# Second layer's state-input projection in four column tiles, its three-way split on 128 columns, the parts spread by small DMAs, a two-input multiply by D, and new instruction orders

## The reference, cut to what matters

```python
xn = _layernorm(x);  x = x + attention(xn) + mixture_of_experts(xn)      # first layer
xn = _layernorm(x);  x = x + state_space(xn) + gated_mlp(xn)             # second layer

def state_space(x, W_in, conv_w, conv_b, A_log, D, W_x, W_dt, b_dt, W_out):
    xs, z = split(x @ W_in)                      # 256 channels each
    xs = silu(causal_conv(xs, conv_w) + conv_b)
    dt = softplus(xs @ W_dt + b_dt)
    Bs = xs @ W_x                                # 16 states per token
    def step(h, inp):                            # h: 256 channels x 16 states
        dt_t, Bs_t, x_t = inp
        h = h * exp(-exp(A_log) * dt_t[..., None]) + Bs_t[:, None, :]
        return (h, sum(h, axis=-1) + D * x_t)
    y = scan(step) * silu(z)
    return y @ W_out
```

## Time and profile before

| what | value |
|---|---|
| device time, median of 3 runs | 382.94 us |
| span of the profiled execution (first to last instruction) | 381.6 us |
| instructions | 5772 |
| TensorE busy | 368.0 us (96%) |
| ScalarE busy | 317.8 us (83%) |
| VectorE busy | 303.0 us (79%) |
| GpSimd busy | 252.4 us (66%) |
| granted TensorE clock | 1.000 of full speed |

### The profile page before, as it was taken

The page is one execution under the profiler, slowest core; times in us unless marked ns, Lnnn a source line. Parts: engine busy times, 40 slices in busy tenths (PEclk is TensorE's granted clock), DMA queues, the critical chain, the costliest instruction groups (busy, mean ns, idle before and its releaser), DMA issues.

```text
span 381.6 us, 5772 instructions
## 1 busy us (share of the span) xinstructions
PE 368.0 (96%) x1762; PEld 184.9 (48%) x1762; DVE 303.0 (79%) x508; ACT 317.8 (83%) x541; POOL 252.4 (66%) x293
## 2 busy tenths in 40 slices
PE   7999999999999999999998899999999999899996
PEld 5667535455545453333344334654445544374545
DVE  4877878878788879469999589989999879686850
ACT  4924879787879887899999799999999999999450
POOL 2245814614515111636899983999999999999880
PEclk9999999999999999999999999999999999999999
DMA  5273875734555310000000000000000000000000
GB/s 208 74 163 117 164 188 157 130 58 103 154 114 120 73 24 3 2 0 1 0 0 3 1 0 0 2 27 1 1 2 0 0 28 3 0 0 1 29 0 27
DMA packets 27726, 18.84 MB, mean 49 GB/s; under 512 B 2832, under 2 KB 26672, under 8 KB 27440
## 3 DMA queue, kind: packets, MB, share of 16 engines
q1 hardware_dynamic: 27696, 18.48, 20.0%
HBM read 13.29 MB, written 4.98 MB: 48 GB/s over the span
## 4 chain that ended last, share of the span: by engine, by line
PE 40%; issue 33%; POOL 13%; ACT 9%; DVE 4%; DMA 1%; POOLq 1%; ACTq 0%; DVEq 0%
POOL acc L1212 9%; PE bank L361 7%; PE bank L346 5%; PE bank L332 5%; PE bank L392 4%; PE bank L400 4%; DVE hb L1157 3%; ACT da L1082 3%; ACT pt L552 3%; PE bank L455 2%; PE bank L321 2%; PE bank L461 1%; PE bank L928 1%; POOL y L1220 1%; PE bank L418 1%
## 5 line engine op out<-in xcount | busy, mean ns | idle before, releaser
L1212 POOL TENSOR_TENSOR acc<-acc,hb 128x512 f32<-128x512 f32 x128 | 158.3, 1268 | 22.1 <-DVE hb L1157 17.5
L1157 DVE TENSOR_TENSOR_SCAN hb<-da,bank 128x512 f32<-128x512 f32 x128 | 146.3, 1201 | 22.6 <-PE bank L864 17.8
L593 DVE TENSOR_REDUCE mx<-bank 128x2 f32<-128x512 f32 x128 | 83.6, 685 | 22.4 <-PE bank L332 18.5
L552 ACT ACTIVATE pt<-bank 128x512 f32<-128x512 f32 x128 | 71.4, 596 | 16.2 <-PE bank L346 13.8
L1082 ACT ACTIVATE da<-dt,nega 128x510 f32<-128x510 f32 x128 | 82.5, 714 | 0.2
L903 PE MATMUL bank<-gelu,ld 128*128 128x512 f32 x128 | 58.3, 593 | 1.1 <-ACT gelu L1063 1.1
L891 PE MATMUL bank<-sil,ld 128*128 128x512 f32 x128 | 58.7, 594 | 0.0
L346 PE MATMUL bank<-q_st,k_st 51*128 51x512 bf16 x128 | 42.4, 383 | 1.5 <-ACT pt L552 1.3
L332 PE MATMUL bank<-k_st,q_st 48*128 48x256 bf16 x240 | 39.3, 273 | 0.0
L903 PEld LDWEIGHTS bank<-gelu,ld 128*128 128x128 f32 x128 | 24.0, 190 | 27.8 <-issue 26.0
L891 PEld LDWEIGHTS bank<-sil,ld 128*128 128x128 f32 x128 | 23.9, 190 | 25.4 <-issue 24.0
(11 more groups left out here) (149 smaller groups left out, 565.2 us busy)
## 6 DMA issues: line engine op xcount, KB each, us to landing
q_st<-q_scr SPq DMA_DIRECT2D x8, 384.0 KB, 4.5
q_st<-q_scr SPq DMA_DIRECT2D x15, 192.0 KB, 4.2
ld<-in_pack SPq DMA_DIRECT2D x2, 1024.0 KB, 6.2
q_scr<-qk_parts SPq DMA_DIRECT2D x8, 192.0 KB, 2.8
k_st<-k_scr SPq DMA_DIRECT2D x15, 96.0 KB, 4.4
q_scr<-qk_parts SPq DMA_DIRECT2D x8, 128.0 KB, 1.9
out<-x SPq DMA_DIRECT2D x8, 128.0 KB, 1.9
ld<-in_pack SPq DMA_DIRECT2D x1, 968.0 KB, 5.7
```

The costliest lines, as they stand in the source:

```text
L552: act(pt[:, n % 8, :], st(b, n)[:, :], ACT.Exp, scale=HD ** -0.5).then_inc(p_ok, 1)
L593: eng.tensor_reduce(mx[:, 2 * pair:2 * pair + 2, q], s_bank[n % 2][:, :].rearrange("p (h k) -> p h k", h=2), AX.X, ALU.max).then_inc(mx_ok, 1)
L1157: eng.tensor_tensor_scan(hb[:, s % NPAIR, c, :], da(n).rearrange("p b n -> p (b n)"), b_bank(g, s)[:, :], 0.0, ALU.mult, ALU.add).then_inc ...
L1212: TT(acc[:, g % 2, c, :], acc[:, g % 2, c, :], hb[:, s % NPAIR, c, :], ALU.add).then_inc(add_ok, 1)
```

## The change

- `wx_p` is 128x32: one copy of W_x. `wx` is eight matmuls: for each c, four of 128 tokens each, whose results go to partitions 32j to 32j+31 and the same 128 columns of the bank. So Bs of 512 tokens lies as 128 partitions (4 blocks of tokens x 32) x 128 columns.
- `b_in` copies 128x128 instead of 96x512, twice, to `b_cut[:, 0, :]` (bf16) and `b_full`.
- `split` is three operations on 128x128 instead of four on up to 96x512. It now also waits until the DMAs of the group before have read `b_cut`.
- `b_rows` is new on SP: for each part p, four DMAs copy 32 rows x 128 columns (8 KB, rows of 256 B) from `b_cut` to their place in `b_parts`. Twelve for a group, 48 in all. Part 0 waits for `b_in`, part 1 for the second operation of `split`, part 2 for the third. The first `b` of a group waits for all twelve.
- `start` multiplies by D as a two-input operation (D broadcast along the tokens) instead of by a scalar for each partition.
- `constants` makes one copy of W_x instead of three.
- All five orders are new. Each holds the same pieces as often as before; SP's also has the 12 `b_rows`. `warm` is still 44 times in TensorE's, but 21 of them, not 9, stand ahead of the first transposes.

```diff
-        wx_p=sb("wx_p", [P, CI, NPART * 32]),
+        wx_p=sb("wx_p", [P, CI, 32]),
...
+        def b_rows(g, p):
+            if p == 0:
+                reached(eng, bx_ok, g, 1, 1)
+                reached(eng, b_ps, g - 2, NS, NS)
+            else:
+                reached(eng, bsp, g, NBS, p + 1)
+            for j in range(GTT):
+                eng.dma_start(b_parts[32 * p:32 * p + 32, g % 2, j * P:(j + 1) * P],
+                              b_cut[32 * j:32 * j + 32, p, :]).then_inc(b_put, 16)
...
-                reached(eng, bsp, g, NBS, NBS)
+                reached(eng, b_put, g, NBP, NBP)
...
-                last = mm(pA[0:NPART * 32, :], wx_p[:, c, :], xs[:, g % 2, c, :],
-                          start=(c == 0), stop=(c == CI - 1))
+                for j in range(GTT):
+                    last = mm(pA[32 * j:32 * j + 32, 0:P], wx_p[:, c, :], xs[:, g % 2, c, j * P:(j + 1) * P],
+                              start=(c == 0), stop=(c == CI - 1))
...
-            act(b_parts[:, g % 2, :], pA[0:NPART * 32, :], ACT.Copy, scale=scale)
-            act(b_full[:, :], pA[0:NPART * 32, :], ACT.Copy, scale=scale).then_inc(bx_ok, 1)
+            act(b_cut[:, 0, :], pA[:, 0:P], ACT.Copy, scale=scale)
+            act(b_full[:, :], pA[:, 0:P], ACT.Copy, scale=scale).then_inc(bx_ok, 1)
...
-            eng.tensor_scalar(acc[:, g % 2, c, :], xs[:, g % 2, c, :], d[:, c:c + 1], None, ALU.mult).then_inc(acc_in, 1)
+            TT(acc[:, g % 2, c, :], xs[:, g % 2, c, :], d[:, c:c + 1].broadcast_to([P, GT]), ALU.mult).then_inc(acc_in, 1)
...
+            reached(eng, b_put, g - 1, NBP, NBP)
+            TT(b_rest[:, :], b_full[:, :], b_cut[:, 0, :], ALU.subtract).then_inc(bsp, 1)
...
+            eng.tensor_copy(b_cut[:, 1, :], b_rest[:, :]).then_inc(bsp, 1)
...
+            TT(b_cut[:, 2, :], b_rest[:, :], b_cut[:, 1, :], ALU.subtract).then_inc(bsp, 1)
```

More of the change, by code:

```diff
@@ L72 @@
 ORDERS = dict(
[L73 to L86, removed]
-        v_gate ffn_in A S A S pv S A S A pv A S A S ffn_out heads A S A pv A S A S back x_transposes A S A pv A
-        S A proj_out S A S A x_in A S A pv max_rows x_in ffn x_in pv A x_in A ffn A wx A ffn 2*step_in A heads b
-        x_transposes ffn A pv A b x_in A x_in A second b second A x_in b A pv back A second b A second x_in b A
-        wx A proj_out b pv A step_in 2*b pv step_in heads b second back b second b 2*second b proj_out third b
-        2*third b third b third x_transposes third b third b third x_in b ffn b x_in ffn x_in b 2*ffn x_in wx
-        2*second b out b step_in b out second b 4*out x_transposes b 2*second 2*b 2*second x_in second 2*b
-        step_in 2*third b third b x_in b 2*third b 2*third b third x_in b ffn b ffn b x_in ffn 2*out ffn 2*b wx
-        2*second b 3*out b second b 2*second b 2*second b out b second 2*step_in 2*b 2*third b third b 2*third
-        2*b 3*third ffn b ffn b out ffn b ffn b 2*out b out 3*second b 2*second b 2*second b second b 2*out
-        third b 2*third b third b 4*third 6*out""",
@@ L122 @@
-    gpsimd="""ones biased 2*G biased 4*G qk_split 2*G qk_split maxima_split 8*G biased qk_split maxima_split 8*G
-        maxima_split qk_split constants 8*G maxima_split G qk_split 7*G maxima_split qk_split 8*G maxima_split
-        qk_split 8*G maxima_split shifted 8*G maxima_split 2*start split 9*add start 3*add start 2*add split
-        14*add shifted 4*add 2*y 18*add start add split 2*add start 11*add 2*y 8*add 2*start 14*add split 11*add
-        y 4*add y 26*add y add y""",
+    sync="""2*x_in head ffn_weights constants0 x_in 3*put fetch 2*put stack put fetch put rows 2*put 2*rows stack loads
+        fetch 3*rows put stack put loads put fetch 3*rows 2*put stack loads put fetch 3*rows 3*put stack fetch put
+        3*rows 2*put stack fetch 3*rows 3*put fetch stack 3*rows stack 3*rows 2*b_rows loads 4*b_rows out 3*b_rows
+        out 2*b_rows out b_rows 5*out landed""",
@@ new lines @@
+    gpsimd="""G biased ones 3*G qk_split 2*G biased 2*G qk_split maxima_split 8*G maxima_split qk_split 4*G biased 2*G
+        maxima_split 2*G qk_split G constants 2*G maxima_split 5*G qk_split 8*G maxima_split qk_split 8*G
+        maxima_split qk_split 8*G shifted maxima_split 8*G maxima_split split 2*start 9*add start 16*add split 3*add
+        start shifted 4*add y add y 15*add start 6*add split add start 10*add 2*y 10*add split 9*add start 11*add y
+        add start add y 31*add 2*y""",
```

99 lines of the change are left out of this document (55 added, 44 removed).

## The result

The changed kernel took 391.94 us (median of 4 runs, 390.66 to 396.14) against 382.93 for the kernel before: a ratio of 1.0244, 95% interval 1.0209 to 1.0280. The forecast was 378.9 us, its range 373.8 to 384.2; the time lies outside it, on the other side of no change. The profiled execution has a span of 389.8 us and a time of 391.59. The ratios in this document leave out runs that lie more than 1.5% above the fastest of their kernel, so a ratio can differ from that of the medians.

The account below looks back on a forecast made before the run. TensorE was taken as the bound, relief of other engines counting only in its gaps. Projection -4.9, gaps -3.0, first `b` +2.9, start +1.0 gave -4.0 us: 378.9 us, range 373.8 to 384.2.

Parts of the forecast that it names:

- The rest of the first layer: First layer behind its start: same work in another order, no gain or loss, 2 us to either side.
- the start: More `warm` matmuls ahead of the first transposes, and later constants: 1.0 us lost, between 0 and 3.
- the first `b`: Group 0 of the second layer: TensorE stands 3.3 us for its parts; 2.9 us lost, ends 1.0 and 8.
- small transfers behind the load come in only with its end: At group 0's `b_rows`: the four DMAs of part 2 land about 0.4 us behind the 1 MB load.
- the second layer without it: Less TensorE projection work (-4.9 us) and relief of GpSimd and ScalarE in TensorE's gaps (-3.0 us).
- the wait without the load: At `b` 0: with no 1 MB load between the twelve DMAs, TensorE would wait 1.0 us.
- TensorE's projection: `wx`: column tiles run side by side, 0.5 us each instead of 1.72, 4.9 us less in all.
- GpSimd and ScalarE: `split`, D's multiply, `b_in` and table loads: 12.7 us less work on GpSimd, 10.3 less on ScalarE.
- the bound of TensorE's gaps: From 160 to 340 us: relief of other engines is worth at most 7.0 us; 3.0 taken.
- Rival (c): Slower, by a longer wait for parts at `b` 0 or a first layer losing 2 us: 384 to 387.3 us; chance 0.18.

Follow-up runs that it names:

- the pairs with and without the filler: 24 unread matmuls added ahead of the first `b`'s wait in two reordered variants of the changed kernel: 379.48 to 377.31 us, and 380.25 to 377.56 us.
- first_b_later: The changed pieces under the old orders, with TensorE's first `b` moved behind the transposes and the ffn that followed it: 380.04 us, ratio 0.9903.
- new_pieces_old_orders: All changed pieces, with the five engine orders of the kernel before (`b_rows` added to SyncE's): 382.53 us, ratio 0.9958.
- D alone: The kernel before with only D's multiply in its two-input form: 380.89 us, ratio 0.9935.

## Why the prediction was wrong

**The step that failed** is this one: "The rest of the first layer has the same work in another order; I find no reason for a gain or a loss, with 2 us to either side." At the first maximum 2.0 us were lost, which belongs to the start, and at the last one 10.6; the 8.6 between are this step's. The rule that would have shown it was in the prediction itself, where it priced the first `b`: "small transfers behind the load come in only with its end". The same rule, laid on the rest of SyncE's list in the diff, gives a load directly ahead of a batch's last `put` or of its fetch three times in batches 2 to 4. The list before has loads ahead of `put`s too, but only the smallest (559 KB) stood directly ahead of a batch's last `put`, the one that the fetch waits for, and that one landed after 3.1 us. Behind the next two, SyncE issued the next `put` 3.6 and 4.5 us later; the fourth stood ahead of the first of a batch's three, and a transfer 1.9 us behind it took 4.4 us where the fetch had two more `put`s to wait for. Moving three entries took 7.5 to 8.8 us off, and in the profiled runs it brought the last maximum from 155.1 to 148.9 us. With the fetch ahead of the stack as well it came at 145.9, 1.4 us behind the kernel before, under the new orders of the other four engines; so in that run all of the first layer's loss behind its start is gone.

The whole in the prediction's terms, forecast against measured: start +1.0 and +2.0, rest of the first layer 0 and +8.6 (with 0.2 more up to the end of the first projection), first `b` +2.9 and +4.2, the second layer without it -7.9 and -6.8. The sums are -4.0 and +8.2. The -7.9 count the first projection's own 1.1 us, which lies ahead of the first scan.

**The granted clock** was priced nowhere. The prediction counted a wait of TensorE at its own length. In the changed kernel the waits at 62 to 66 us (2.2 us) and 176 to 179.6 us (3.57 us) were followed by about 6 and about 10 us at 0.50. What such a stretch costs is what the pairs with and without the filler show, where the filler does nothing for the arrival of the parts: 2.3 and 2.7 us in the two pairs that are clear of noise. In the second pair the mean clock is 0.986 without the filler and 1.000 with it, over 379 us, which makes some 10 us at the half level (2 x 0.014 x 379). So about a quarter of such a stretch came back and not half of it.

**The first `b`**: right in mechanism. The load stood between parts 1 and 2, issues took 0.59 us and not 0.53, TensorE stood for 3.57 us (3.3 forecast). The term of +2.9 us was too small: the first scan came 12.9 us behind the first projection where it had been 8.7, so 4.2 us later, with some 10 us at half clock behind it. The forecast of 1.0 us for the wait without the load was right: in first_b_later, where the same work stands ahead of `b`, it was 0.68 us. The 2.8 us of new_pieces_old_orders don't speak against it, since `b` stands 2.1 us of work sooner there.

**TensorE's projection**: right. 0.65 us each (0.5 forecast), 4.3 us in all (4.9).

**GpSimd and ScalarE**: right or too careful in the pieces. Split 1.15 us (1.1 without waits), table loads 46 (46), b_in 0.27 and 0.28 us (0.261). D's multiply was costed at the 1.268 us of an add and measured 1.04; the second operand is one value for each partition, repeated. Of the estimates that the prediction worked out from the Trainium skill (GPSIMD Engine Reference, section 3.1), that of the two-input form is near the trace, 1.11 against 1.04 us, and that of the one-input form isn't, 0.44 against 1.558.

**What relief is worth**: no run went over the bound of TensorE's gaps, 7.0 us, but 3.0 us for 23 us of relief was near the low side. D alone gave 2.5 us, and the second layer from its first scan on became 6.8 us shorter in the changed kernel, with a falling clock still in it. The forecast's sum for it without the first `b`, -4.9 - 3.0 = -7.9, is close to that.

**The start**: 42 matmuls ended at 8.78 us (7.9 to 9.9 forecast), the first transposes ran at 8.62, and the first maximum came at 16.3 instead of 14.3 us; the term of +1.0 was 2.0 by then. What it was worth by itself wasn't tried.

Rival (c), the slower one, named both right causes, "the wait for the parts at `b` 0" and "new orders that lose 2 us in the first layer", and stopped at 387.3 us, for want of the loads' place and of the clock. Its own price for the wait, issues of 1.78 us behind the load, didn't come: the four took 0.51 and 0.59 us.

What stays open: how much of the first three loads' 7.5 to 8.8 us is wait and how much is clock, since no run filled those gaps; why the clock fell behind some waits of 1 to 2 us and not behind others of 2; and one DMA for each part instead of four wasn't tried.

## What to carry to other kernels

When a diff moves entries in a queue's list, go through the whole list, and for each large transfer ask which small transfer is issued within the next few microseconds and who waits for it; and ask the same of its own deadline. A wait of TensorE for some microseconds can cost more than its length, since the clock may fall behind it: fill it with work that could run, or with matmuls that nobody reads (2.3 and 2.7 us back here, on waits of 1.9 and 1.4 us). Test the pieces and the orders of a change apart: here the pieces were good, the new second-layer orders were good, and the places of a few transfers in one list hid both.

## What the runs showed of the hardware

- A small transfer to scratch issued 1.0 to 1.3 us behind a load of 968 KB or 1 MB on the same queue landed after 6.0 to 6.9 us, 1.8 us behind it after 3.9, and with no load near it after 1.6 to 2.0.
- A gap of 1.67 us in TensorE's work was followed by 8 us at a granted clock of 0.50; with a gap of 0.69 us at the same place the clock stayed at 1.00. In the changed kernel it stayed at 1.00 behind gaps of 2.04 and 1.81 us too, so the length of the gap alone doesn't decide it.
- On GpSimd a multiply by a repeated operand of one value for each partition took 1.04 us on 128x512, an add of two full operands 1.27, and the one-input form with a scalar for each partition 1.558.
